# A multi-head latent attention with a gated FFN on one core: rope tables kept in SBUF, one copy of the keys, heads in turn, rope swap by ScalarE copies

## Chip, cores and metric

The kernel runs on one core of a Trainium2 chip. The metric is the device time of one execution in microseconds (us), the median of several runs. TensorE (PE), VectorE (DVE), ScalarE (ACT) and GpSimd (POOL) each run their own instruction stream in order; SyncE (SP) issues the DMAs. Semaphores tie the streams together. The whole program is written out by hand, so nothing but the order of the code sets the order on an engine.

## What is computed

```python
x = L0_attn_x                                    # (1, 2048, 256), float32
xn = layernorm(x)
s = attn(xn, ...)                                # 16 heads, causal, 2048 x 2048
g = silu(ffn(xn, ...))                           # gate and up 704 x 256, down 256 x 704
out = x + s * g

# attn: NOPE, ROPE, VD, LORA = 128, 64, 128, 64
q_nope, q_pe = split(x @ wq)                     # per head 128 + 64
ckv, k_pe = split(x @ wkv_a)                     # 64 + 64
ckv = rmsnorm(ckv) * kv_norm_scale
k_nope, v = split(ckv @ wkv_b)                   # per head 128 + 128
q_pe, k_pe = rope(q_pe), rope(k_pe)              # [x1*cos - x2*sin, x2*cos + x1*sin], halves of 32
scores = (concat(q_nope, q_pe) @ concat(k_nope, k_pe).T) * 192 ** -0.5, causal
out = softmax(scores) @ v, heads side by side, @ wo
```

## The kernel before

**Form.** The products of weights are folded, so that queries and keys have 128 rows: 64 of the latent space and 64 of rope. Keys are then the same for all heads. Float32 accuracy comes from splitting each operand into a high and a low part and adding three products (hi x hi, hi x lo, lo x hi). Queries (QA, QB for the two heads of a pair), keys (KA, KB) and x lie transposed in SBUF, each as hi and lo, 2048 columns. Head A has its rope rows on partitions 0 to 63 and its latent rows on 64 to 127, head B the other way round, so there are two copies of the keys.

**Units.** The 16 heads go as 8 pairs. A pair has 16 units (PU), a unit u does one head and two query tiles of 128 rows, tile 15 - k and tile k, against all keys at or below the diagonal: 17 key tiles whatever k is. It falls into three pieces m: m = 0 the first 1024 keys of the high tile, m = 1 the rest of the high tile, m = 2 the low tile. Before, head A has units 0 to 7 of a pair and head B units 8 to 15.

**One unit, by engine.** PE computes scores(u, m) into five banks of PSUM (s_ps, one set only); DVE takes the row maxima; ACT the exponentials (prob) and the high half of them in 16 bits (hl); the low half is made by POOL for m = 0 (`prob_low`, named low(u)) and by DVE for m = 1, 2. SP then issues two DMA transposes, turn_first(u) for m = 0 and turn_rest(u) for m = 1, 2, which turn hi and lo from hl into pT; PE multiplies pT by the values two units later (weigh, LAG = 2) and DVE normalises. In one turn of the loop PE does scores(u+1, 0), scores(u+1, 1), weigh(u-2, 0), scores(u+1, 2), the rest of weigh, and the jobs of u. ACT does exp(u, 0), exp(u, 1), hi(u, 0), exp(u, 2), the jobs of u-1, hi(u, 1), hi(u, 2). DVE normalises u-3, takes the maxima (u+1, 0) and (u+1, 1), does the jobs of u-1, low (u, 1) and (u, 2), and the maximum (u+1, 2). POOL does low(u) and then the steps of u. The waits: a score bank is free once its exponential is done; prob0 is single, so exp(u+1, 0) waits for low(u); hi(u) waits for the transpose of u-2.

**Jobs and steps.** The tables JOBS_*, with at most two jobs a unit, say at which unit PE, ACT and DVE do the small work of the pair itself, of the pair before (projection outT, outP) and of the next one: wqT, wkvT and wabs make the folded weights, `pe{g}` the rope rows of both heads for group g of 512 queries (PE 6 matmuls, ACT a copy into q_pe), `lat{g}` the latent rows of both heads (PE 6 matmuls, ACT two copies QA_hi, QB_hi, DVE two subtractions). POOL_* place POOL's steps: rope{g}.0 multiplies q_pe by cosT, rope{g}.1 q_swap by sinT, rope{g}.2 adds; then the sides A{g}hi, A{g}lo, B{g}hi, B{g}lo go into the query tiles. wpe_hi, wpe_lo and wkvs prepare weights. Groups go in the order 3, 0, 2, 1.

**SP's queue.** In order: turn_first(u), then, where they fall, `swap(g)` (four DMAs of 32 rows that write q_pe with its halves exchanged into q_swap), `load_tables` (cosT and sinT of the next group, 128x512 each; SBUF holds one group), turn_rest(u), and at k = 0, 11 the loads of the next pair's weights (wq_sb and wkvs, wo_sb).

## Time and profile before

| | us |
|---|---|
| median of 3 runs (1116.97 to 1122.3) | 1118.76 |
| profiled execution | 1120.68 |
| its span in the profile | 1118.9 |
| PE, DVE, ACT, POOL busy | 985.6, 831.2, 714.0, 662.8 |
| first transposes of pairs 0, 1, 7; of the last unit | 79.5, 208.7, 898.3; 997.4 |

The span is the time from the first to the last instruction. The attention runs from the setup (to about 70 us) to about 1007 us, the FFN fills the rest. The page gives busy time by engine, the chain that ended last and groups of instructions; stretches of time can be asked for by themselves, and so can the waits of one engine for another. An instruction of a DMA queue is an issue: the transfer lands some us later. A busy PE isn't a PE at its peak, since matmuls overlap.

### The profile page before, as it was taken

The numbers are of one execution on the slowest core, as the hardware profiler recorded it, in microseconds if no ns is written. First come the engines' busy times: TensorE is split into PE (matmuls) and PEld (weight loads), VectorE is DVE, ScalarE is ACT, GpSimd is POOL, SyncE is SP. The second block draws the span as 40 slices with busy tenths as digits, with TensorE's granted clock in tenths as the row PEclk, the third lists the DMA queues.
The fourth block names the chain that finished last, engine by engine and source line by source line (L and its number), as shares of the span: only waits on it lengthen the run. The fifth ranks groups of instructions, "written<-read, shape, count | busy, mean of one in ns | idle before, by whom it ended". The sixth has DMA issues, their size and how long they took to land.

```text
span 1118.9 us, 26420 instructions
## 1 busy us (share of the span) xinstructions
PE 985.6 (88%) x10576; PEld 842.8 (75%) x10576; DVE 831.2 (74%) x1359; ACT 714.0 (64%) x1033; POOL 662.8 (59%) x448
## 2 busy tenths in 40 slices
PE   6864898989988988999889998998899986989998
PEld 5743787778777877788778877876688775878887
DVE  6674687988787877878798779887888885873134
ACT  1335567776676767677677677776677774863232
POOL 3736766766576675756685658565857684422331
PEclk7777899999999999899999999999999998999999
DMA  5118899999999999999999999999999899992001
GB/s 146 38 40 168 152 186 197 197 197 184 184 187 199 189 187 185 202 184 188 189 207 185 197 190 206 180 192 178 202 178 211 179 192 207 178 176 76 1 20 57
DMA packets 600042, 184.92 MB, mean 165 GB/s; under 512 B 574960, under 2 KB 586864, under 8 KB 599920
## 3 DMA queue, kind: packets, MB, share of 16 engines
q1 hardware_dynamic: 595440, 182.57, 89.6%
q8 instruction: 84, 1.38, 0.5%
q10 hardware_dynamic: 4480, 0.66, 0.4%
q14 instruction: 38, 0.31, 0.1%
HBM read 30.09 MB, written 2.10 MB: 29 GB/s over the span
## 4 chain that ended last, share of the span: by engine, by line
PE 34%; DMA 24%; DVE 17%; POOL 10%; SPq 6%; ACT 5%; issue 4%; ACTq 1%; POOLq 0%
DMA pT<-hl 19%; PE s_ps L637 12%; PE s_ps L535 9%; DVE hl L948 5%; PE slot_ps L535 5%; DVE part_max L939 5%; POOL hl L1099 5%; ACT hl L743 3%; DMA sinT<-sinT_dram 2%; SPq L464 2%; ACT prob L809 2%; PE o_ps L653 2%; SPq L477 2%; PE o_ps L535 2%; PE o_ps L654 2%
## 5 line engine op out<-in xcount | busy, mean ns | idle before, releaser
L1099 POOL TENSOR_TENSOR hl<-prob,hl 128x1024 f16<-128x1024 f32 x128 | 274.5, 2144 | 228.3 <-ACT hl L743 224.4
L743 ACT ACTIVATE hl<-prob 128x1024 f16<-128x1024 f32 (+7 forms) x384 | 295.9, 804 | 160.3 <-DMA pT<-hl 159.6
L809 ACT ACTIVATE prob<-s_ps,neg_max 128x1024 f32<-128x1024 f32 (+7 forms) x384 | 316.7, 859 | 101.4 <-DVE neg_max L942 46.6
L939 DVE TENSOR_REDUCE part_max<-s_ps 128x1 f32<-128x1024 f32 (+7 forms) x256 | 243.7, 985 | 93.4 <-PE s_ps L637 74.4
L948 DVE TENSOR_TENSOR hl<-prob,hl 128x1024 f16<-128x1024 f32 (+7 forms) x256 | 255.9, 1035 | 62.4 <-ACT hl L743 62.1
L653 PE MATMUL o_ps<-v,pT 128*128 128x65 f16 x2176 | 231.8, 194 | 51.0 <-DMA pT<-hl 39.3
L653 PEld LDWEIGHTS o_ps<-v,pT 128*128 128x128 f16 x2176 | 205.4, 97 | 58.0 <-DMA pT<-hl 45.9
L654 PE MATMUL o_ps<-v,pT 128*128 128x64 f16 x2176 | 232.2, 196 | 0.0
L655 PE MATMUL o_ps<-v,pT 128*128 128x65 f16 x2176 | 231.1, 193 | 0.0
L655 PEld LDWEIGHTS o_ps<-v,pT 128*128 128x128 f16 x2176 | 205.6, 100 | 0.0
L654 PEld LDWEIGHTS o_ps<-v,pT 128*128 128x128 f16 x2176 | 204.8, 98 | 0.0
L637 PE MATMUL s_ps<-KA_hi,QA_hi 128*128 128x512 f32 (+3 forms) x320 | 129.0, 403 | 36.6 <-ACT prob L809 21.1
L637 PE MATMUL s_ps<-KB_hi,QB_hi 128*128 128x512 f32 (+3 forms) x320 | 125.0, 391 | 6.8 <-ACT prob L809 6.7
L637 PE MATMUL s_ps<-KA_lo,QA_hi 128*128 128x512 f32 (+3 forms) x320 | 120.7, 377 | 0.0
L637 PE MATMUL s_ps<-KA_hi,QA_lo 128*128 128x512 f32 (+3 forms) x320 | 120.2, 376 | 0.0
L637 PE MATMUL s_ps<-KB_hi,QB_lo 128*128 128x512 f32 (+3 forms) x320 | 117.4, 367 | 0.0
L637 PE MATMUL s_ps<-KB_lo,QB_hi 128*128 128x512 f32 (+3 forms) x320 | 117.3, 367 | 0.0
L637 PEld LDWEIGHTS s_ps<-KA_hi,QA_hi 128*128 128x128 f32 x320 | 63.3, 198 | 56.1 <-ACT prob L809 30.2
L937 DVE TENSOR_REDUCE neg_max<-s_ps 128x1 f32<-128x128 f32 (+7 forms) x128 | 95.4, 745 | 11.8 <-PE s_ps L640 11.8
L1231 POOL TENSOR_TENSOR hid_lo<-hid,hid_hi 128x512 fp32r<-128x512 f32 x24 | 31.4, 1307 | 75.5 <-ACT hid_hi L743 75.5
L637 PEld LDWEIGHTS s_ps<-KB_hi,QB_hi 128*128 128x128 f32 x320 | 60.8, 190 | 19.7 <-ACT prob L809 9.9
L1099 POOL TENSOR_TENSOR q_swap<-q_swap,sinT 128x512 f32<-128x512 f32 x32 | 45.1, 1409 | 47.1 <-DMA q_swap<-q_pe 45.7
(196 smaller groups left out, 1985.5 us busy)
## 6 DMA issues: line engine op xcount, KB each, us to landing
cosT<-cosT_dram SPq DMA_DIRECT2D x32, 256.0 KB, 4.0
sinT<-sinT_dram SPq DMA_DIRECT2D x32, 256.0 KB, 4.1
q_swap<-q_pe SPq DMA_DIRECT2D x128, 64.0 KB, 2.1
pT<-hl SPq DMA_TRANSPOSE x256, 5.2
wq_sb<-in_L_attn_wq_dram SPq DMA_DIRECT2D x8, 384.0 KB, 3.9
acc<-in_L_attn_x_dram SPq DMA_DIRECT2D x4, 512.0 KB, 6.5
wo_sb<-in_L_attn_wo_dram SPq DMA_DIRECT2D x8, 256.0 KB, 3.7
x_in<-in_L_attn_x_dram SPq DMA_DIRECT2D x1, 2048.0 KB, 8.5
```

Of the source, the lines that this page charges most:

```text
L535: last = nc.tensor.matmul(out_ap, a, b, start=(i == 0), stop=(i == n - 1))
L637: mm = nc.tensor.matmul(s_ps[:, b, 0:c], a[head][:, q], kk[head][:, k0 + c0:k0 + c0 + c], start=(j == 0), stop=(j == 2 and not ends))
L653: nc.tensor.matmul(whole, pT[:, b, :], v[:, kb, 0:LORA + 1], start=(m != 1 and b == 0), stop=False)
L654: nc.tensor.matmul(part, pT[:, b, :], v[:, kb, LORA + 1:VW], start=False, stop=False)
L655: last = nc.tensor.matmul(whole, pT[:, n + b, :], v[:, kb, 0:LORA + 1], start=False, stop=(m > 0 and b == n - 1))
L743: return nc.scalar.activation(dst, src, ACT.Copy)
L809: nc.scalar.activation(prob_of(u, m), score_bank(u, m), ACT.Exp, bias=neg_max[:, r:r + 1]).then_inc(exp_done, 1)
L937: nc.vector.tensor_reduce(neg_max[:, r:r + 1], src, AX.X, ALU.max, negate=True).then_inc(max_ready, 1)
L939: nc.vector.tensor_reduce(part_max[:, u % 2, m:m + 1], src, AX.X, ALU.max).then_inc(part_done, 1)
L948: nc.vector.tensor_tensor(both[:, w:2 * w], prob_of(u, m), both[:, 0:w], ALU.subtract).then_inc(lo_dve, 1)
L1099: return lambda: nc.gpsimd.tensor_tensor(dst, a, b, op)
L1231: nc.gpsimd.tensor_tensor(hid_lo[:, n % 2, it, :], hid[:, j % 2, :], hid_hi[:, n % 2, it, :].bitcast(F32), ALU.subtract).then_inc(hid_lo_d ...
```

## The change

- **Tables.** cosT and sinT become 128x2048 and are loaded once, in four parts, in the setup. TABLES_AT and the reloads go.
- **Rows.** Both heads have rope rows on 0 to 63 and latent rows on 64 to 127, so one copy of the keys (K_hi, K_lo) does, with 4 key jobs in the setup in place of 8. The weights for both parts lie in one tile, wc_hi, wc_lo.
- **Query jobs.** `q{A,B}{g}` takes the place of `pe{g}` and `lat{g}`: one job for each head and group, again 6 matmuls. ACT makes four copies of its result: rope rows into q_pe, the two halves of 32 rows in exchanged order into q_swap, latent rows into the queries. The swap DMAs go. DVE makes one low part a job.
- **Rope.** For head B the last addition moves to DVE (`rope_of_b`, from partitions 64 to 127 into pe_b on 0 to 63); POOL's covers head A alone. q_pe and q_swap get two buffers.
- **Heads in turn.** Unit u has head u % 2 and step k = u % 16 // 2; groups 3 and 0 serve units 0 to 7 of a pair, 2 and 1 units 8 to 15. The normalised output goes into o_tiles, two buffers of four tiles. All job and step tables are written anew.
- **Setup.** qA3, qB3, qA0, qB0 replace pe3, pe0, lat3, lat0; POOL does B3 and B0 before the first unit.

```diff
 def head_of(u):
-    return u // HALF % 2
+    return u % 2
-JOBS_BEFORE = {0: ["outP0a", "outP0b"], 1: ["outT1"], 3: ["outP1a", "outP1b"], 4: ["outT2"], 6: ["outP2a", "outP2b"],
-               7: ["outT3"], 9: ["outP3a"], 10: ["outP3b"]}
-JOBS_OWN = {10: ["wvo"], 14: ["outT0"]}
-JOBS_NEXT = {2: ["wqT"], 5: ["pe3"], 7: ["wkvT"], 8: ["pe0"], 9: ["wabs"], 11: ["pe2", "lat3"], 12: ["lat0"], 13: ["pe1"],
-             14: ["lat2"], 15: ["lat1"]}
+JOBS_BEFORE = {2: ["outT3"], 4: ["outP3a", "outP3b"]}
+JOBS_OWN = {0: ["qA2"], 1: ["qB2"], 2: ["qA1"], 3: ["qB1"], 5: ["wvo"], 6: ["outT0"], 7: ["outP0a", "outP0b"], 10: ["outT1"],
+            12: ["outP1a", "outP1b"], 14: ["outT2"], 15: ["outP2a", "outP2b"]}
+JOBS_NEXT = {3: ["wqT"], 5: ["wkvT"], 6: ["wabs"], 8: ["qA3"], 9: ["qB3"], 10: ["qA0"], 11: ["qB0"]}
...
-POOL_NEXT = {2: ["wpe_hi"], 3: ["wpe_lo"], 4: ["wkvs"], 7: rope(3)[:2], 8: [rope(3)[2], "A3hi"], 9: ["A3lo"], 10: rope(0)[:2],
...
+POOL_NEXT = {1: ["wkvs"], 6: ["wpe_hi"], 7: ["wpe_lo"], 10: rope(3)[:1], 11: rope(3)[1:] + ["A3hi"], 12: ["A3lo", rope(0)[0], "B3hi"],
...
-                for name in jobs_at(u - 1):
-                    if name[0].startswith("pe"):
-                        swap(int(name[0][2:]), name[1])
-                if u in TABLES_AT:
-                    load_tables(*TABLES_AT[u])
...
-                    copy(QA_hi[LORA:P, c], ps[LORA:P, :])
-                    copy(QB_hi[0:LORA, c], ps[0:LORA, :]).then_inc(hi_done, 1)
-                    copy(q_pe[:], ps).then_inc(act_freed, 1)
+                    n = group_no(g, pair)
+                    if n >= 2:
+                        before = GROUP_ORDER[(n - 2) % NG], (n - 2) // NG
+                        act.wait_ge(pool_done, POOL.after((f"rope{before[0]}.2", before[1])))
+                        act.wait_ge(rope_b, n - 1)
+                    half = ROPE // 2
+                    copy(q_pe[h * ROPE:(h + 1) * ROPE, n % 2, :], ps[0:ROPE, :])
+                    copy(q_swap[h * ROPE:h * ROPE + half, n % 2, :], ps[half:ROPE, :])
+                    copy(q_swap[h * ROPE + half:(h + 1) * ROPE, n % 2, :], ps[0:half, :])
+                    copy(queries(Q_hi, h, g)[ROPE:P, :], ps[ROPE:P, :]).then_inc(hi_done, 1)
...
+                nc.vector.tensor_tensor(pe_b[:, n % 2, :], pe[ROPE:P, n % 2, :], q_swap[ROPE:P, n % 2, :], ALU.add).then_inc(rope_b, 1)
```

On SP's queue, in pair 0 before (hl0 and pT0 belong to turn_first, hl12 and pT12 to turn_rest):

```order
L470 DMA_TRANSPOSE pT0<-hl0 128x16x128
L464 DMA q_swap<-q_pe 32x512 x4
L477 DMA_TRANSPOSE pT12<-hl12 128x18x128
L470 DMA_TRANSPOSE pT0<-hl0 128x16x128
L477 DMA_TRANSPOSE pT12<-hl12 128x18x128
L470 DMA_TRANSPOSE pT0<-hl0 128x16x128
L451 DMA cosT<-cosT_dram 128x512
L452 DMA sinT<-sinT_dram 128x512
L477 DMA_TRANSPOSE pT12<-hl12 128x18x128
```

and now, at the change from pair 0 to pair 1:

```order
L446 DMA_TRANSPOSE pT0<-hl0 128x16x128
L453 DMA_TRANSPOSE pT12<-hl12 128x18x128
L416 DMA wq_sb<-in_L0_attn_wq_dram 128x2x384
L417 DMA wkvs<-in_L0_attn_wkv_b_dram 64x512
L446 DMA_TRANSPOSE pT0<-hl0 128x16x128
L453 DMA_TRANSPOSE pT12<-hl12 128x18x128
L446 DMA_TRANSPOSE pT0<-hl0 128x16x128
L453 DMA_TRANSPOSE pT12<-hl12 128x18x128
```

Between two transposes there is nothing left but the loads of weights. On ACT, one turn of the loop in pair 0 before, with the jobs pe2 and lat3 of the next pair in it:

```order
L809 ACTIVATE prob12<-s_ps,neg_max 128x512
L743 ACTIVATE hl0<-prob0 128x1024
L809 ACTIVATE prob12<-s_ps,neg_max 128x640
L743 ACTIVATE q_pe<-slot_ps 128x512
L743 ACTIVATE QA_hi<-slot_ps 64x512
L743 ACTIVATE QB_hi<-slot_ps 64x512
L743 ACTIVATE hl12<-prob12 128x512
L743 ACTIVATE hl12<-prob12 128x640
```

and now, with the query job of one head (QB21 holds head B's groups 2 and 1):

```order
L772 ACTIVATE prob12<-s_ps,neg_max 128x896
L706 ACTIVATE hl0<-prob0 128x1024
L772 ACTIVATE prob12<-s_ps,neg_max 128x256
L706 ACTIVATE q_pe<-slot_ps 64x512
L706 ACTIVATE q_swap<-slot_ps 32x512 x2
L706 ACTIVATE QB21_hi<-slot_ps 64x512
L706 ACTIVATE hl12<-prob12 128x896
L706 ACTIVATE hl12<-prob12 128x256
```

The exchanged copies stand between exp(u, 2) and the two halves of the unit, and such a block now comes in eight units of a pair. On POOL the scaling of the next pair's wkvs stood five low halves behind the pair's start; now it stands right behind the second:

```order
L1080 TENSOR_TENSOR hl0<-prob0,hl0 128x1024 x2
L1080 TENSOR_TENSOR wkvs<-wkvs,scale_sb 64x512
L1080 TENSOR_TENSOR hl0<-prob0,hl0 128x1024
L1080 TENSOR_TENSOR pe<-q_pe,cosT 128x512
L1080 TENSOR_TENSOR hl0<-prob0,hl0 128x1024
```

The load of wkvs is issued by SP behind turn_rest of the pair's unit 0, as before.

## Rows read from the trace of the kernel before

**Rows 1.** Stretches: start:end, length, busy us and instructions (x) by engine.
```profile
core 0: us, PE busy (x) PEld busy (x) DVE busy (x) ACT busy (x) POOL busy (x), PEclk, DMA share, GB/s
79.50:208.70 129.20, 105.70 (x1141) 89.51 (x1140) 91.23 (x145) 87.06 (x124) 84.66 (x57) 0.89 0.93 176
208.70:898.30 689.60, 629.83 (x7357) 534.69 (x7355) 568.07 (x903) 499.09 (x709) 455.24 (x282) 0.98 1.07 191
961.90:997.30 35.40, 34.42 (x480) 30.50 (x478) 33.13 (x62) 30.84 (x47) 12.89 (x7) 1.00 1.21 191
```
**Rows 2.** Timeline of SP's queue, pair 4: start us, duration us, issue.
```profile
576.36 1.94 SPq L470 DMA_TRANSPOSE pT<-hl  x1
578.39 4.01 SPq L477 DMA_TRANSPOSE pT<-hl  x1
582.50 1.80 SPq L470 DMA_TRANSPOSE pT<-hl  x1
...
594.12 1.76 SPq L470 DMA_TRANSPOSE pT<-hl  x1
595.97 3.06 SPq L464 DMA_DIRECT2D q_swap<-q_pe  x4
...
601.95 3.14 SPq L470 DMA_TRANSPOSE pT<-hl  x1
```
**Rows 3.** Timeline of POOL, same place: the low half low(68).
```profile
575.60 2.15 POOL L1099 TENSOR_TENSOR hl<-prob,hl 128x1024 f16<-128x1024 f32 x1
```
**Rows 4.** Waits, 208.7 to 898.3 us: total us, times, longest.
```profile
ACT hl L743 <- DMA pT<-hl: 140.7, 78, 4.7
...
POOL q_swap L1099 <- DMA q_swap<-q_pe: 37.7, 11, 4.4
```
**Rows 5.** The page's DMA issues: count, KB each, median us to landing.
```profile
wkvs<-in_L_attn_wkv_b_dram SPq DMA_DIRECT2D x8, 128.0 KB, 3.9
```
**Rows 6.** Groups by shape on ACT, 208.7 to 898.3 us: busy us, mean ns | idle before.
```profile
L743 ACT ACTIVATE QA_hi<-slot_ps 64x512 fp32r<-64x512 f32 x24 | 14.2, 593 | 1.3 <-PE slot_ps L535 0.8
...
L743 ACT ACTIVATE q_pe<-slot_ps 128x512 f32<-128x512 f32 x24 | 14.2, 591 | 0.2 <-PE slot_ps L535 0.2
```
**Rows 7.** Timeline of ACT in the setup: copies in a row.
```profile
51.46 0.58 ACT L743 ACTIVATE KB_hi<-s_ps 128x512 fp32r<-128x512 f32 x1
51.94 0.59 ACT L743 ACTIVATE KA_hi<-s_ps 128x512 fp32r<-128x512 f32 x1
```
**Rows 8.** Groups by shape on DVE, 208.7 to 898.3 us.
```profile
L948 DVE TENSOR_TENSOR hl<-prob,hl 128x512 f16<-128x512 f32 x24 | 30.4, 1268 | 6.3 <-ACT hl L743 6.3
...
L896 DVE TENSOR_TENSOR QB_lo<-slot_ps,QB_hi 64x512 fp32r<-64x512 f32 x24 | 16.4, 682 | 0.3
```
**Rows 9.** Timeline of SP's queue, end of pair 7.
```profile
961.96 3.14 SPq L470 DMA_TRANSPOSE pT<-hl  x1
...
970.19 2.97 SPq L477 DMA_TRANSPOSE pT<-hl  x1
...
997.36 1.99 SPq L470 DMA_TRANSPOSE pT<-hl  x1
```
**Rows 10.** Timeline of POOL, same place: low(123).
```profile
970.68 2.15 POOL L1099 TENSOR_TENSOR hl<-prob,hl 128x1024 f16<-128x1024 f32 x1 [3.49 <-ACT hl L743]
```
**Rows 11.** Groups on POOL, 208.7 to 898.3 us.
```profile
L1099 POOL TENSOR_TENSOR pe<-q_pe,cosT 128x512 f32<-128x512 f32 x24 | 31.5, 1313 | 25.1 <-DMA sinT<-sinT_dram 23.6
...
L1099 POOL TENSOR_TENSOR wkvs<-wkvs,scale_sb 64x512 f32<-64x512 f32 x6 | 8.3, 1388 | 0.5
```
**Rows 12.** Timeline of ACT, end of pair 7: exp(124, 0), in brackets idle time before.
```profile
974.15 1.11 ACT L809 ACTIVATE prob<-s_ps,neg_max 128x1024 f32<-128x1024 f32 x1 [1.25 <-DVE neg_max L942]
```
**Rows 13.** Timelines of POOL and DVE in the setup.
```profile
40.94 1.28 POOL L1099 TENSOR_TENSOR pe<-q_pe,cosT 128x512 f32<-128x512 f32 x1 [1.15 <-issue]
...
67.25 0.67 DVE L886 TENSOR_TENSOR KA_lo<-s_ps,KA_hi 128x512 fp32r<-128x512 f32 x1
```
**Rows 14.** Waits, 79.5 to 208.7 us.
```profile
PE s_ps L637 <- POOL QA_lo L1099: 11.4, 1, 11.4
```
**Rows 15.** Waits of the whole span, at the load of the FFN weights.
```profile
POOL up_raw L1099 <- DMA down_scale<-in_L_ffn_down_s_dram: 13.3, 1, 13.3
```

280 lines of the change are left out of this document (129 added, 151 removed).

## Prediction

> **What bounds the kernel now.** I read the stretches first, then the queue of SyncE, then who waits for whom, then the durations.
>
> The stretches [rows 1] cut the span at the first transposes of head pairs 0, 1 and 7. Pairs 1 to 6 (96 units, a unit being one head and two query tiles) take 689.6 us, 7.18 us a unit or 114.9 us a pair. In them DVE is busy 568.07 us (5.92 a unit), ACT 499.09 (5.20), POOL 455.24 (4.74), PE 629.83 (6.56). PE's figure is too high as a floor: its records last longer than the distance to the next start, so each tail of a group counts. No engine is full, the DMA share is 1.07.
>
> SyncE's queue [rows 2] shows what is full. From 576.36 to 594.12 us it issues only transposes, back to back, three units in 17.76 us or 5.92 a unit. The next unit has four swaps in the queue (3.06 us) and takes 601.95 - 594.12 = 7.83 us. GpSimd had the low halves of the unit whose first transpose starts at 582.50 ready at 575.60 + 2.15 = 577.75 [rows 3]: the transpose is 4.7 us late, with everything computed. So the queue is behind, and the swaps and table loads stand in it. The waits agree [rows 4]: ACT, which may not overwrite a half before the transpose of two units earlier has landed, waits 140.7 us for that in pairs 1 to 6; GpSimd waits 37.7 us for swaps and 23.6 us for tables [rows 4, 11]. **The in-order DMA path sets the pace of the attention, and every engine trails it.**
>
> **Removed from the queue.** Per pair four loads of cosT and of sinT, and four times four swaps; they stand in eight of its 16 units. The unit with swaps was 1.9 us longer than the three without. If every one of the eight units a pair with swaps or tables costs 1.9 to 2.3 us, that is 15 to 18 us a pair; 16 x 5.92 = 94.7, plus 2 to 3 us for the two loads that stay, gives a DMA path of 97 to 98 us a pair after the change. That is the fastest a pair can be. Of each table 28 of 32 loads go, and all 128 swaps; four loads of each remain in the setup.
>
> **Added on ScalarE.** Before, a query group costs three copies (q_pe, QA_hi, QB_hi), after it eight (for each head q_pe, two of 32 rows, and the upper half of the queries). That is 5 more a group, 20 a pair. A copy of 512 columns takes 591 ns [rows 6], and copies in a row start 0.48 us apart [rows 7]; the columns, not the rows, are the same in 128- and 64-row copies (591 and 593 ns), and I take the 32-row ones as equal. So 20 x 0.48 to 0.59 = 9.6 to 11.8 us a pair; ACT goes from 499.09/6 = 83.2 to 93 to 95 us a pair. It sits between exp(u, 2) and the halves (u, 1), (u, 2), in 8 of 16 units. Behind it on ACT stand those halves, behind them DVE's low parts and the second transpose, and the next unit's exponentials. [...]
>
> **Added on VectorE.** One addition a group (rope_of_b, 64x512, two SBUF inputs), 4 a pair. The nearest rows [rows 8] are a subtraction of the same size with one input in PSUM, 682 ns, and the low part of 512 columns with both inputs in SBUF, 1268 ns on average. I take 1.0, 4.0 us a pair, with 2.7 and 5.1 us as ends. The query low parts stay two a group. DVE goes from 568.07/6 = 94.7 to 98.7 us a pair. The Trainium skill (SBUF — State Buffer, Who interferes with whom) says why the two rows may differ: an operation of VectorE with two SBUF inputs and one of GpSimd that reads SBUF exclude each other, the later waits. By it every addition would meet GpSimd and cost 1.3 us: 1.2 us a pair more than I count, 1054 in place of the forecast.
>
> **GpSimd.** The same steps with the same shapes. Its waits for swaps and tables (61.3 us in pairs 1 to 6) go; they were slack. What is new: the scaling of wkvs moves from step 4 to step 1 of a pair, right behind low(1), while its load is still issued behind the second transpose of unit 0. The load lands 3.9 us after its issue [rows 5], and stands behind the issue of wq (some 0.6 us). In the free stretch at the end the second transpose of a unit has been issued at 970.19 + 2.97 = 973.16, and the next unit's low half ends at 970.68 + 2.15 = 972.83 [rows 9, 10]. So GpSimd stands 0.3 + 0.6 + 3.9 = 4.8 us, then scales for 1.4 [rows 11]: 6.2 us, where a unit of 6.6 us leaves 6.6 - 2.15 = 4.4 beside the low half. low(2), and behind it the overwriting of prob0 by exp(3, 0), come 1.8 us late. From 972.83 to the exponential that needed it at 974.15 there was 1.3 us of slack [rows 10, 12]; I count 1 us a pair, between 0 and 3.
>
> **TensorE.** Six matmuls of 512 columns a job, two jobs a group, as before (per head now, where it was rope and latent). The order of heads changes which tiles come when, and not how many. The queries of groups 2 and 1 are now wanted from unit 8 of a pair, not from unit 4.
>
> **What a pair then takes.** The stretch from 961.90 to 997.30 us [rows 1] is the kernel without swaps, tables and next pair's work. First transposes start at 961.96 and 997.36 [rows 9], with six units between them, 5.90 us each. DVE is busy 33.13 of 35.4 us there, 94%, PE 97%. So the engines can be packed to 94% of DVE when the DMA path isn't behind. 98.7 / 0.936 = 105.4; with 1 us for wkvs, **106 us a pair**, 6.6 a unit. ACT is then 89% busy and the DMA path has 8 us a pair to spare. From PE's side: 629.83/6 = 105.0 us with its tails, 108 at 97%, an upper bound that fits.
>
> **Setup, first and last pair.** In the setup the rope of group 3 starts at 40.94 us [rows 13]. Now it needs the job of both heads, which waits for wabs, after two kv jobs; GpSimd stands about 10 us and then has rope (3 x 1.3), two key blocks, rope again before DVE can end, where it ended at 67.25 + 0.67 us [rows 13]. Against that stand four key jobs, with their copies, which go. I take +3 us, between 0 and +8. Pair 0 took 129.2 us; its one long hole is PE waiting 11.4 us for QA_lo [rows 14], because group 2 was wanted at unit 4. Now it has until unit 8. Pair 0 at 106: -23. Pair 7 (99 us before) gets the four jobs of its own groups 2 and 1 and some output jobs from the end, about +4; the hole at the load of the FFN weights, where GpSimd waited 13.3 us [rows 15], gets a unit more of lead, about -3. Together +1. The FFN stage I leave as it is.
>
> **Sum.** 1118.9 + 3 - 23 - (689.6 - 636) + 1 = 1046 us of span. The profiled execution was 1120.68 us, 1.8 over its span and 1.9 over the median of 1118.76; so 1046 also stands for the median of the runs.
>
> **The rivals.**
> (A) The forecast, 1046, DVE and PE near full: 0.52.
> (B) The engines pack tighter and the DMA path stays the bound at 98 us a pair. Seven pairs at 8 us less: 1046 - 56 = 990. For: half the units carry light jobs, and buffers are two deep. Against: DVE would be 98.7/98, over full. Only with 0.68 us additions and shorter low parts does it come near, so 0.08, and then nearer to 1005.
> (C) ScalarE bound in its eight full units. ACT's work in a unit is about 83.2/16 = 5.2, less the old copies (12 x 0.48 a pair, 0.36), so 4.8 without any group work; four copies make 6.8, with an outT or wqT copy 7.3, and waits for neg_max (1.25 us before an exponential in the free stretch, [rows 12]) on top. Eight units at 7.6, eight at 6.2: 110 us a pair. 1046 + 7 x 4 = 1074. For: the scores have one set of banks, so what delays an exponential delays the next scores. Against: ACT can run ahead of DVE by the two buffers of its halves. 0.28.
> (D) No change, 1119: the swaps and tables were hidden and the transposes' own rate sets 7.2 us. The 5.92 us stretch excludes it nearly: 0.03.
> (E) Slower. The loop exp -> scores -> maximum -> exp already needs 5.9 us, and the copies, which stand in it on ACT, are not absorbed at all, with q jobs on PE waited for as well. It decides from (114.9 - 8 x 6.1)/8 = 8.3 us for a unit with a query job. At 8.5 (5.9 + 4 x 0.59 and 0.25 of waits) a pair has 117: pairs 1 to 6 +12, pair 0 -12, pair 7 +9, setup +3: 1119 + 12 = 1131. 0.05. A worse tail of C, between 1085 and 1113, has the remaining 0.04.
>
> **How the numbers follow.** Forecast 1046. The range goes from 1005 (B at its likely end) to 1086 (C with a pair at 111.5). A measurement of this kernel can tell about 0.5% from no change. Faster by over 0.5% (under 1113): A, B, C and the tail, 0.92; within 0.5%: D, 0.03; slower: E, 0.05.
>
> **What would show it.** The SyncE queue should have no table load or swap after the setup, and a transpose should start within 1 us of its low part in most units; ACT's wait for pT should fall from 140.7 us to under 40. First transposes of pairs should stand 106 us apart, DVE over 90% busy, ACT near 89%. If ACT is the bound, DVE's waits for ACT hl grow and units with four copies are 1 us and more longer than the others. GpSimd should wait for wkvs once a pair, 3 to 5 us. First transpose of pair 0 near 82 us, the next pair's near 188. Wrong it would be if the transposes alone, with the queue free of the rest, still ran at 7 us a unit, or if ACT waited for PE's query jobs in each of the eight units.

## The result, and the profile after

| | before | after |
|---|---|---|
| median of four runs each | 1117.87 us (1115.93 to 1122.30) | 1132.87 us (1127.33 to 1133.82) |
| ratio to before, 95% interval | | 1.012 (1.009 to 1.015) |
| the profiled execution, its span | 1120.68, 1118.9 us | 1133.82, 1132.0 us |

The changed kernel is 1.2% slower. The forecast was 1046 us, the range ended at 1086; both are wrong, and so is the sign. The number that came out is the one that the prediction gave to its rival E, 1131 us at 117 us a pair; whether for E's reasons is told below. Single executions that took over 1.5% longer than the fastest of the same kernel (one each of d1, d2 and e1, the last at a granted clock of 0.555 and 1511.8 us) are left out of every median and ratio.

The stretches of the changed kernel, cut at the first transposes of pairs 0, 1 and 7 as in [rows 1] (start:end, length, busy us and instructions by engine, granted clock, DMA share, GB/s):

```profile
core 0: us, PE busy (x) PEld busy (x) DVE busy (x) ACT busy (x) POOL busy (x), PEclk, DMA share, GB/s
88.40:202.80 114.40, 103.02 (x1131) 86.21 (x1130) 97.80 (x146) 94.34 (x137) 77.29 (x47) 0.95 0.96 162
202.80:904.00 701.20, 625.65 (x7322) 528.86 (x7322) 617.59 (x925) 568.73 (x828) 455.28 (x282) 0.99 0.94 161
904.00:1010.30 106.30, 92.53 (x1149) 79.34 (x1149) 91.44 (x148) 83.55 (x121) 60.58 (x35) 0.95 1.01 177
```

The first transpose comes at 88.4 us (79.5 before). Pair 0 takes 114.4 us (129.2). Pairs 1 to 6 take 701.2 us, 116.9 a pair (689.6, 114.9). DVE is busy 102.9 us a pair where it was 94.7, ACT 94.8 where it was 83.2. GpSimd is as before. The DMA share has fallen from 1.07 to 0.94.

Who waits for whom, whole span (us in total, times, longest):

```profile
POOL hl L1080 <- ACT hl L706: 253.0, 103, 7.5
ACT prob L772 <- DVE neg_max L910: 112.2, 78, 3.9
...
ACT prob L772 <- DVE neg_max L915: 63.9, 35, 13.6
...
PE o_ps L617 <- DVE o_tiles L933: 58.1, 40, 2.6
...
POOL wkvs L1080 <- issue: 17.9, 4, 5.8
...
ACT hl L706 <- DMA pT<-hl: 6.1, 2, 5.8
...
POOL up_raw L1080 <- DMA down_scale<-in_L_ffn_down_s_dram: 6.0, 1, 6.0
```

The wait that bounded the old kernel, ACT for landed transposes [rows 4], is gone: 140.7 us in pairs 1 to 6 alone, now 6.1 us in the whole span. In its place ScalarE waits for VectorE's maxima, and TensorE for VectorE's o_tiles. The page's chain of work that ended last says the same:

```profile
DVE 27%; PE 25%; ACT 21%; issue 14%; POOL 8%; DMA 2%; SPq 1%; ACTq 1%; POOLq 0%
```

SyncE's queue has gaps now. Over pairs 1 to 6 its issues fill 509 of 701 us, where they filled 658 of 690. A few of them (start us, duration us):

```profile
455.31 2.56 SPq L453 DMA_TRANSPOSE pT<-hl  x1
458.26 1.93 SPq L446 DMA_TRANSPOSE pT<-hl  x1
463.11 2.68 SPq L453 DMA_TRANSPOSE pT<-hl  x1
465.88 2.94 SPq L446 DMA_TRANSPOSE pT<-hl  x1
471.09 2.40 SPq L453 DMA_TRANSPOSE pT<-hl  x1
```

Between the end of one issue at 460.19 and the next start at 463.11 it waits for a low part. By the trace's start and end times a unit's first transpose now starts 0.9 us behind its low half on average, and 67 of 96 start within 1 us; before it was 4.5 us, and 1 of 96. Against [rows 2], where transposes stood back to back, the queue has been freed, as the prediction said. What happens instead in this place is on ScalarE and VectorE. ScalarE, from one exponential of unit 52 to the next of unit 53, 7.99 us, with idle time before in brackets:

```profile
460.38 1.91 ACT L772 ACTIVATE prob<-s_ps,neg_max 128x1024 f32<-128x1024 f32 x2
462.17 1.05 ACT L706 ACTIVATE hl<-prob 128x1024 f16<-128x1024 f32 x1
463.70 0.58 ACT L772 ACTIVATE prob<-s_ps,neg_max 128x384 f32<-128x384 f32 x1 [0.48 <-DVE neg_max L910]
464.31 0.59 ACT L706 ACTIVATE q_pe<-slot_ps 64x512 f32<-64x512 f32 x1
464.91 1.18 ACT L706 ACTIVATE q_swap<-slot_ps 32x512 f32<-32x512 f32 x2
466.11 0.59 ACT L706 ACTIVATE QB_hi<-slot_ps 64x512 fp32r<-64x512 f32 x1
466.73 0.60 ACT L706 ACTIVATE wqT<-slot_ps 128x512 f32<-128x512 f32 x1
467.22 1.25 ACT L706 ACTIVATE hl<-prob 128x768 f16<-128x768 f32 x2
468.37 1.90 ACT L772 ACTIVATE prob<-s_ps,neg_max 128x1024 f32<-128x1024 f32 x2
```

Four copies of a query job run from 464.31 to the start of the next at 466.73: 2.42 us, 0.60 apart and not 0.48 as the full-height copies of [rows 7]. VectorE at two pairs of low parts over the same 1152 columns, and GpSimd at the second:

```profile
452.69 2.01 DVE L921 TENSOR_TENSOR hl<-prob,hl 128x896 f16<-128x896 f32 x2 [0.28 <-ACT hl L706]
...
460.07 3.00 DVE L921 TENSOR_TENSOR hl<-prob,hl 128x896 f16<-128x896 f32 x2 [0.28 <-ACT hl L706]
```
```profile
459.67 1.28 POOL L1080 TENSOR_TENSOR pe<-pe,q_swap 64x512 f32<-64x512 f32 x1
461.03 1.77 POOL L1080 TENSOR_TENSOR QA_hi<-pe,ones 64x512 fp32r<-64x512 f32 x1
```

The second pair has GpSimd's steps beside nearly all of it (from 460.07 to 462.80, and it ends at 463.07) and takes 3.00 us; GpSimd's own step takes 1.77 us there, where the same form took 1.03 at its least. The cost of GpSimd to VectorE's low parts, which the prediction had only inside one average (1268 ns, [rows 8]), turned out to be one of the main terms (a3, d3 and f1 below).

### The profile page after: what moved, and what is told of

Its sections match the earlier page's. It is cut to its first block, busy times and chain, and to the rows that moved or that the text cites. A ratio compares the mean times of both kernels' runs of the same rounds, so it can differ in the third digit from the quotient of the medians.

```text
span 1132.0 us, 26361 instructions
## 1 busy us (share of the span) xinstructions
PE 985.5 (87%) x10560; PEld 838.2 (74%) x10560; DVE 896.3 (79%) x1383; ACT 806.2 (71%) x1189; POOL 666.9 (59%) x448
## 4 chain that ended last, share of the span: by engine, by line
DVE 27%; PE 25%; ACT 21%; issue 14%; POOL 8%; DMA 2%; SPq 1%; ACTq 1%; POOLq 0%
DVE hl L921 12%; PE s_ps L503 9%; PE s_ps L601 8%; ACT hl L706 7%; ACT prob L772 6%; DVE part_max L912 5%; ACT q_swap L706 4%; DVE neg_max L910 4%; POOL hl L1080 4%; PE slot_ps L503 3%; DVE acc L884 2%; PE o_ps L503 2%; ACT q_pe L706 2%; DVE pe_b L869 1%; DMA scale_sb<-_attn_kv_norm_scale_dram 1%
## 5 line engine op out<-in xcount | busy, mean ns | idle before, releaser
L921 DVE TENSOR_TENSOR hl<-prob,hl 128x768 f16<-128x768 f32 (+7 forms) x256 | 280.1, 1133 | 6.4 <-ACT hl L706 4.3
L601 PE MATMUL s_ps<-K_hi,QA_hi 128*128 128x512 f32 (+3 forms) x320 | 129.1, 403 | 25.0 <-ACT prob L772 17.3
L601 PE MATMUL s_ps<-K_hi,QB_hi 128*128 128x512 f32 (+3 forms) x320 | 126.6, 396 | 14.1 <-ACT prob L772 14.0
L601 PE MATMUL s_ps<-K_hi,QA_lo 128*128 128x512 f32 (+3 forms) x320 | 119.9, 375 | 0.0
L601 PE MATMUL s_ps<-K_lo,QA_hi 128*128 128x512 f32 (+3 forms) x320 | 119.6, 374 | 0.0
L601 PE MATMUL s_ps<-K_hi,QB_lo 128*128 128x512 f32 (+3 forms) x320 | 119.3, 373 | 0.0
L601 PE MATMUL s_ps<-K_lo,QB_hi 128*128 128x512 f32 (+3 forms) x320 | 118.6, 371 | 0.0
L910 DVE TENSOR_REDUCE neg_max<-s_ps 128x1 f32<-128x256 f32 (+7 forms) x128 | 96.2, 752 | 1.9
L601 PEld LDWEIGHTS s_ps<-K_hi,QA_hi 128*128 128x128 f32 x320 | 62.3, 195 | 46.9 <-ACT prob L772 30.6
L706 ACT ACTIVATE q_swap<-slot_ps 32x512 f32<-32x512 f32 x122 | 71.7, 588 | 1.4
```

The source lines that it names most:

```text
L601: mm = nc.tensor.matmul(s_ps[:, b, 0:c], a[:, q], kk[:, k0 + c0:k0 + c0 + c], start=(j == 0), stop=(j == 2 and not ends))
L706: return nc.scalar.activation(dst, src, ACT.Copy)
L910: nc.vector.tensor_reduce(neg_max[:, r:r + 1], src, AX.X, ALU.max, negate=True).then_inc(max_ready, 1)
L921: nc.vector.tensor_tensor(both[:, w:2 * w], prob_of(u, m), both[:, 0:w], ALU.subtract).then_inc(lo_dve, 1)
```

## The experiments

Theory V: VectorE is the bound of the changed kernel, through its additions and through low parts slowed by GpSimd. Theory S: ScalarE's copies are. A third possibility is that the floor under both, 106 us a pair, was itself wrong. All times below are medians, with the ratio to the kernel before measured beside them and its 95% interval; "a pair" is the distance of the first transposes of pairs 1 and 7 by six, from the trace of one execution. Rows of stretches have the columns of the first table above.

### One or the other addition taken away

a1_no_add: VectorE's addition over 8 columns.

```diff
-nc.vector.tensor_tensor(pe_b[:, n % 2, :], pe[ROPE:P, n % 2, :], q_swap[ROPE:P, n % 2, :], ALU.add)
+nc.vector.tensor_tensor(pe_b[:, n % 2, 0:8], pe[ROPE:P, n % 2, 0:8], q_swap[ROPE:P, n % 2, 0:8], ALU.add)
```

> The changed kernel with VectorE's new addition (rope_of_b) over 8 columns in place of 512, so the rope rows of head B are left out (they stay the zeros of a memset in the setup); all waits and all other instructions stay. Theory V (VectorE is the bound of the changed kernel: the additions and low parts slowed by GpSimd): 4 additions of 1.23 us a pair go, 32 in all = 39 us, nearly all on the path, so 1095 to 1100 us. Theory S (ScalarE's copies are the bound in the units with query jobs): VectorE only follows, 1125 to 1133 us.

Measured: 1101.6 us, 0.979 (0.977 to 0.982), a pair 112.6 us.

a2_no_swap_copies: ScalarE's exchanged copies over 8 columns.

```diff
-copy(q_swap[h * ROPE:h * ROPE + half, n % 2, :], ps[half:ROPE, :])
-copy(q_swap[h * ROPE + half:(h + 1) * ROPE, n % 2, :], ps[0:half, :])
+copy(q_swap[h * ROPE:h * ROPE + half, n % 2, 0:8], ps[half:ROPE, 0:8])
+copy(q_swap[h * ROPE + half:(h + 1) * ROPE, n % 2, 0:8], ps[0:half, 0:8])
```

> The changed kernel with the second eviction in exchanged order (four copies of 32 rows a query group, 16 a pair) over 8 columns in place of 512; the sine part of the rope is left out with it, all waits stay. 16 x 0.60 us = 9.6 us a pair go, less what an 8-column copy still takes (some 0.2 us each), so about 6.5 us a pair or 50 us in all. Theory S: most of it is on the path, 1080 to 1095 us. Theory V: VectorE stays full, and at most 10 us go, 1122 to 1133 us.

Measured: 1100.0 us, 0.978 (0.974 to 0.982), a pair 112.9 us.

a3_neither: both edits.

> Both edits at once: VectorE's addition and ScalarE's exchanged copies over 8 columns each. What is left is the changed kernel's order with its free SyncE queue and nothing added. If one of the two theories holds alone, this gives what its own run gives. If the two engines take turns as the bound (the units with copies by ScalarE, the others by VectorE), it gives more than the sum of both: under 1060 us. If the order of work itself (GpSimd's steps three to a unit, jobs in rows of units, keys and heads taking turns) costs what the prediction missed, it stays above 1090 us.

Measured: 1070.6 us, 0.951 (0.948 to 0.954), a pair 109.2 us.

Neither theory holds alone, and a3 lies between the cases written down for it (under 1060, over 1090). From the changed kernel (116.9) a1 takes 4.3 us a pair, a2 4.0 and both together 7.7: they nearly add up. The narrowed instructions are not gone. An exchanged copy over 8 columns still took 0.17 us, so ScalarE's busy time over pairs 1 to 6 fell from 568.7 to 528.7 us in a2, 6.7 a pair, and 4.0 of it were on the path. An addition over 8 columns took 0.45 us on average where the full one took 1.15 (1.21 in pairs 1 to 6), and VectorE's busy time fell from 617.6 to 601.3 us in a1, 2.7 a pair: less than the 4.3 that the pair gained.

How that can be is seen in unit 7 of a pair (counted from 0), which gives half of it: between its first exponential and that of unit 8 the changed kernel takes 8.7 us (mean of six), a1 6.5. VectorE and ScalarE there, in pair 3 of the changed kernel:

```profile
481.99 1.58 DVE L869 TENSOR_TENSOR pe_b<-pe,q_swap 64x512 f32<-64x512 f32 x1
483.60 3.67 DVE L921 TENSOR_TENSOR hl<-prob,hl 128x640 f16<-128x640 f32 x2
487.19 0.68 DVE L910 TENSOR_REDUCE neg_max<-s_ps 128x1 f32<-128x512 f32 x1
```
```profile
487.90 0.69 ACT L772 ACTIVATE prob<-s_ps,neg_max 128x512 f32<-128x512 f32 x1 [3.50 <-DVE neg_max L910]
```

The maximum that the last exponential of unit 7 waits for stands on VectorE behind the addition and behind the low parts of unit 6, and these take 3.67 us beside GpSimd. ScalarE stands 3.5 us; in a1 it stands 1.3 us at this place.

The same distances show where the copies count. The eight units of a pair that hold a query job's copies take 7.46 us on average and the other eight 7.15. With the exchanged copies narrowed (a2) they take 6.93 and 7.18, with the additions narrowed (a1) 7.46 and 6.61. Each edit shortened one half of the units, which is why the two nearly add up. The prediction's signs of a full ScalarE are missing: units with four copies should have been 1 us and more longer than the others, and are 0.3 us longer; VectorE's waits for ScalarE's high parts (DVE hl <- ACT hl) should have grown, and fell from 52.9 to 3.4 us over pairs 1 to 6.

What remains in a3, 109.2, is still over the predicted 106; 2.1 us a pair of additions and 2.6 of small copies are left in it.

### The old kernel with its queue freed

b1_free_queue: the kernel before with the tables of group 3 loaded once for all groups, the swaps left out, and q_pe in the place of the swapped rows.

```diff
-                    run((name, pair), tt(q_swap[:], q_swap[:], sinT[:], ALU.mult), (swapped, 64 * (n + 1)))
+                    run((name, pair), tt(q_swap[:], q_pe[:], sinT[:], ALU.mult))
...
-                for name in jobs_at(u - 1):
-                    if name[0].startswith("pe"):
-                        swap(int(name[0][2:]), name[1])
-                if u in TABLES_AT:
-                    load_tables(*TABLES_AT[u])
```

> The kernel before with its SyncE queue freed and nothing put in its place: the tables are loaded once (so later groups take the wrong ones) and the four swaps are left out, GpSimd multiplying q_pe by the sine table with the same shape. If the in-order DMA path alone set its pace, as the prediction has it, a pair falls from 114.9 to about 101 to 106 us and the time to 1045 to 1065 us. If the engines were right behind the queue, at 7 us a unit, it gives 1095 to 1117 us.

Measured: 1056.0 us, 0.939 (0.935 to 0.942), a pair 105.3 us. The first half of the prediction stands: the swaps and loads in the DMA path held the old kernel, and without them a pair is 9.6 us shorter. The stretch of pairs 1 to 6 and the chain of this kernel:

```profile
200.90:832.80 631.90, 608.15 (x7324) 522.49 (x7320) 552.52 (x901) 498.15 (x709) 442.69 (x283) 0.99 1.04 178
```
```profile
PE 54%; DVE 25%; POOL 6%; ACT 5%; issue 5%; DMA 3%; SPq 1%; ACTq 1%; POOLq 0%
```

PE is busy 96% (608.15 of 631.90) and holds 54% of the chain, DVE is busy 87%. So TensorE is the fullest engine here, but 105.3 us a pair is not its floor: f1 below leaves TensorE's work as it is and takes 102.8 us a pair. From the other side, TensorE's matmuls at the median distance between their starts (0.23 us for 512 columns of scores, 0.03 us for the products with the values) come to 96 to 97 us a pair in this kernel, in f1 and in the changed one alike: an estimate from the traces' start times. No run changed TensorE's own work. The changed kernel has PE busy 89% (625.65 of 701.20) and 25% of the chain: it waits more for the other engines.

### GpSimd's steps beside VectorE

d3_less_pool: a3 with GpSimd's 16 split steps a pair over 8 columns from pair 1 on.

```diff
+                m = 8 if pair else BANK
-                src = (pe_b if head else pe)[0:ROPE, n % 2, :]
-                hi, lo = queries(Q_hi, head, g)[0:ROPE, :], queries(Q_lo, head, g)[0:ROPE, :]
+                src = (pe_b if head else pe)[0:ROPE, n % 2, 0:m]
+                hi, lo = queries(Q_hi, head, g)[0:ROPE, 0:m], queries(Q_lo, head, g)[0:ROPE, 0:m]
```

> The changed kernel without its addition and exchanged copies (1070.6 us, 109.2 us a pair), with the 16 split steps of GpSimd a pair over 8 columns in place of 512 from pair 1 on (so these pairs keep old rope rows in most columns). In the changed order GpSimd has three steps behind its low half in 12 of 16 units, and the long units are those. If these runs of steps, through the late low half or through slower low parts of VectorE, are what the changed order costs against the kernel before with a free queue (105.3 us a pair), a pair falls to 105 us or less, 1035 to 1045 us. If it is the extra copy and the small ones on ScalarE, or the order of the jobs, a pair stays at 108 to 109 and the time at 1060 to 1070 us.

Measured: 1040.4 us, 0.928 (0.924 to 0.932), a pair 104.8 us. The two kernels, a3 first, each with all engines and then with the low and high halves (hl) alone, where the busy times are those of DVE, ACT and POOL:

```profile
189.20:844.20 655.00, 607.84 (x7322) 522.12 (x7321) 602.26 (x925) 528.17 (x828) 462.36 (x282) 1.00 1.02 173
```
```profile
189.20:844.20 655.00, 215.79 (x192) 222.21 (x288) 214.58 (x96) 1.00 1.02 173
```
```profile
187.70:816.60 628.90, 609.11 (x7322) 524.13 (x7322) 558.80 (x925) 528.43 (x828) 357.54 (x282) 0.99 1.05 180
```
```profile
187.70:816.60 628.90, 174.45 (x192) 222.34 (x288) 211.25 (x96) 0.99 1.05 180
```

Nothing was taken from VectorE, and its busy time fell by 43.5 us; the low parts (the first figure of the hl rows, DVE) give 41.3 of it. PE is back at 97%. The other way in which GpSimd's steps could cost time, a late low half of its own, did not change: ScalarE's wait for it over pairs 1 to 6 was 11.6 us in a3 and is 13.4 us, while its waits for VectorE's maxima fell from 111.1 to 82.7 us. So work on GpSimd is work on VectorE here. The expectation counts three steps of GpSimd in 12 of 16 units of the changed order; by its step tables it is 8 of 16, against 4 in the old order. Sorting the pairs of low parts of the changed kernel by whether GpSimd ran beside them (from the trace's start and end times, pairs 1 to 6): 36 with GpSimd beside under a tenth of their time took 1.50 us (the two durations added), 12 with GpSimd beside over nine tenths 3.23 us; in a3, 30 took 1.50 and 31 took 3.05.

The same narrowing in the old order: e1_less_pool_before.

> The kernel before with its queue freed (1056.0 us, 105.3 us a pair, wrong tables), with GpSimd's 16 split steps a pair over 8 columns from pair 1 on. In the changed order the same edit gave 4.4 us a pair and took VectorE's low parts from 215.8 to 174.5 us over pairs 1 to 6. If GpSimd's steps cost the same wherever they stand, a pair falls to 101 us and the time to 1028 to 1032 us. If the old order has them where VectorE doesn't meet them, or where the loop is bound otherwise, a pair stays above 103.5 us: 1045 to 1056 us, and the order is what the changed kernel pays for.

Measured: 1039.1 us, 0.926 (0.922 to 0.931), between the two cases. Its trace is that of the execution of 1511.8 us, so the same kernel was traced again as f1_less_pool_before:

> The kernel before with its queue freed and GpSimd's split steps over 8 columns from pair 1 on, once more for its trace. The times gave 14.6 us less than with full steps, about 2.3 us a pair: 103 us. If the steps cost less in the old order because VectorE meets them less, the low parts over pairs 1 to 6 fall from 184.4 us by 10 to 20 us, where they fell by 41.3 in the changed order; if they fall by 40 us here too, it is the loop that does not profit, not the meeting.

One run, 1043.3 us, a pair 102.8 us:

```profile
200.30:817.00 616.70, 605.28 (x7323) 520.11 (x7320) 520.20 (x900) 496.69 (x709) 341.63 (x283) 1.00 1.09 183
```
```profile
200.30:817.00 616.70, 151.20 (x192) 221.94 (x289) 206.31 (x96) 1.00 1.09 183
```

The low parts fell from 184.4 to 151.2 us, by 33 where the changed order gave 41: my 10 to 20 us were wrong, GpSimd meets VectorE nearly as much in the old order. The time gained is 2.5 us a pair against 4.4, and f1 is a single execution. A reading that fits is that the old order has less to gain: PE is busy 98% here, and ScalarE waits for landed transposes again (22.9 us over pairs 1 to 6, 25 times). It was not tested. What the changed order costs is visible in a3 against b1: low parts 215.8 against 184.4 us, with the same GpSimd steps at other places, 30 us more on ScalarE (four full copies a pair more, and the sixteen narrowed ones), and 12.7 us of narrowed additions on VectorE. Together these cost 3.9 us a pair; how the 3.9 divide among them wasn't separated.

### Mending the changed kernel

c1_add_on_pool: head B's addition as a fourth step of GpSimd's rope.

```diff
+                else:
+                    run((name, pair), tt(pe_b[:, n % 2, :], pe[ROPE:P, n % 2, :], q_swap[ROPE:P, n % 2, :], ALU.add))
```

> The changed kernel with head B's rope addition on GpSimd (a fourth step of a group's rope) in place of VectorE; nothing is left out. VectorE loses 32 additions of 1.15 us (37 us), GpSimd gains 32 steps of 1.3 us (42 us) and is busy 63% instead of 59%. With the addition narrowed away the time was 1101.6 us. If what counts is the work on VectorE, this gives 1100 to 1110 us; if more work on GpSimd slows VectorE's low parts as much (both read SBUF), it gives 1115 to 1133 us.

Measured: 1105.8 us, 0.985 (0.981 to 0.989), a pair 113.2 us. It is 3.7 us a pair better than the changed kernel, and the first that leaves nothing out and beats the kernel before. The low parts went up from 213.8 to 225.7 us, 2 us a pair, which is the part of the additions that comes back through GpSimd.

c2_consts_first: table loads held behind the constants.

```diff
+            sp.wait_ge(consts_loaded, 64)
             for g in GROUP_ORDER:
                 load_tables(g)
```

> The changed kernel with SyncE waiting for the four constants before it issues the eight table loads; nothing is left out. In the setup VectorE waited 8.3 us for scale_sb where it had waited 4.3, and the first transpose came at 88.4 where it had come at 79.5. If the 2 MB of tables in front of the constants delay them, the first transpose comes 4 us earlier or more and the time is 1124 to 1129 us. If the setup is late through GpSimd's later start of the ropes alone, nothing changes: 1133 us.

Measured: 1124.3 us (ten runs), 1.003 (1.000 to 1.006). The first transpose comes at 78.6 us, where it was 88.4. The row it goes back to, of the changed kernel, is VectorE's first operation on a constant, and the wait before it:

```profile
20.58 0.29 DVE L991 CAST wkva_hi<-wkva_sb 128x256 fp32r<-128x256 f32 x1 [8.27 <-DMA scale_sb<-_attn_kv_norm_scale_dram]
```

It is 2.9 us in c2. So 2 MB of tables issued ahead delayed the constants; holding them back makes the setup 9.8 us shorter, 5.4 of them in this wait.

f2_pool_and_consts: both.

> The changed kernel with head B's addition on GpSimd and with the table loads behind the constants; nothing is left out. One gave 0.985 of the kernel before, where the changed kernel has 1.012, the other 1.003. One acts in every pair and the other in the setup, so they should add up: 0.974 to 0.980, 1092 to 1098 us. If the setup's gain only moves a wait into pair 0, 0.983 to 0.987.

Measured: 1103.9 us, 0.981 (0.977 to 0.985). They do not add up: 0.985 went to 0.981 and not to 0.976, and the intervals overlap, so it isn't shown that f2 is faster than c1 at all. c1 alone had its first transpose at 84.8, f2 has it at 84.1. VectorE's wait for scale_sb is 3.0 us here and 8.3 in c1, so the constants do come earlier, and the first transpose gains 0.7 us by it. VectorE waits 3.4 us for GpSimd's pe in both; that GpSimd's longer ropes now end the setup fits this, but wasn't tested.

### Other ways to take the swaps off the queue

c3_swap_copies: the kernel before, with the exchanged copies in its old order (q_swap with two buffers), tables still loaded for each group.

```diff
+                    for i in range(4):
+                        copy(q_swap[i * half:(i + 1) * half, n % 2, :], ps[(i ^ 1) * half:(i ^ 1) * half + half, :])
                     copy(q_pe[:], ps).then_inc(act_freed, 1)
```

> The kernel before with ScalarE's four copies of 32 rows in place of the four swaps by DMA, and everything else of it (order of heads, two copies of the keys, tables loaded again for each group); nothing is left out. Without swaps and reloads it took 1056 us. 16 copies of 0.60 us a pair are 9.6 us; in the changed kernel 53 us of such copies cost 33 us, so 72 us cost some 45 us: 1095 to 1105 us, with 0 to 10 us more if the table loads still hold the queue back. If the copies are absorbed as the prediction had it, 1060 to 1075 us.

Measured: 1086.9 us, 0.967 (0.963 to 0.970), a pair 109.2 us. Between the two cases that were expected, and 3.3% faster than the kernel before with this one part of the change. ScalarE does nearly as much as in the changed kernel (554.2 us over pairs 1 to 6 against 568.7), yet its pairs are 7.7 us shorter.

c4_shifted_products: the swap inside GpSimd's product with the sine; GpSimd's steps are placed anew for it.

```diff
+                elif i < 5:
...
+                    a, b = slice((i - 1) * half, i * half), slice((i - 1 ^ 1) * half, (i - 1 ^ 1) * half + half)
+                    run((name, pair), tt(q_swap[a, :], q_pe[b, n % 2, :], sinT[b, :], ALU.mult))
```

> The kernel before with the swap done inside GpSimd's product with the sine table: four products of 32 rows that read one block of rows and write its neighbour, in place of four DMAs and one product of 128 rows; nothing is left out. No copy and no DMA is added; GpSimd gets 12 more steps of 1.3 us a pair (125 us in all, 650 to 775 us busy, 73%). Base is 1056 us, plus 0 to 10 us for the table loads and 8 us for pair 0. If GpSimd has the room that its waits show and VectorE isn't slowed, 1062 to 1080 us. If its steps slow VectorE's low parts, or three steps a unit delay the low halves, 1085 to 1110 us.

Measured: 1090.5 us, 0.970 (0.967 to 0.974), a pair 108.3 us, at the edge of the slower case. No work was added to VectorE, and its low parts rose to 241.2 us over pairs 1 to 6 (184.4 in b1): 9.5 us a pair. ScalarE now waits 77.1 us for GpSimd's low half over the same stretch, where it waits 3.1 us in c3. Twelve products a pair on GpSimd and sixteen copies a pair on ScalarE cost about the same.

d1_tables_by_pool and d2_tables_by_act: c3 with the table loads issued on GpSimd's or on ScalarE's queue.

```diff
+                    if 2 <= n < NG * PAIRS - 1:
+                        nxt = query_cols(GROUP_ORDER[(n + 1) % NG])
+                        pool.wait_ge(pool_done, POOL.after((name, pair)))
+                        pool.dma_start(cosT[:], cosT_in[:, nxt]).then_inc(tables_more, 16)
+                        pool.dma_start(sinT[:], sinT_in[:, nxt]).then_inc(tables_more, 16)
```

> The version with swap copies in the old order (1086.9 us), with the table loads of groups 3 and later issued by GpSimd itself, right behind the product that used the old table; nothing is left out. In that version the four units of a pair with table loads took 7.7, 7.9, 8.6 and 8.0 us where the kernel with the free queue took 5.8, 6.3, 7.5 and 6.8, and the units with swap copies took no longer. If the loads' places in SyncE's queue are what is left, a pair falls from 109.2 to about 105.5 us and the time to 1058 to 1068 us. If it is the copies, 1080 to 1087 us stay.

> The same, with these loads issued on ScalarE's queue behind exp(u, 2); nothing is left out. An issue there took 0.50 us in the setup, eight a pair are 4 us of ScalarE. If ScalarE absorbs this as it absorbs the swap copies in this order, 1060 to 1070 us; if its time counts in full, 1080 to 1095 us.

Measured: 1115.6 us, 0.994 (0.991 to 0.997), a pair 113.6 us, and 1087.9 us, 0.968 (0.962 to 0.975), a pair 110.4 us. Neither helps, and the first costs 29 us. GpSimd's issue, and SyncE's queue at the same place:

```profile
213.97 0.59 POOL L1113 DMA_DIRECT2D cosT<-cosT_dram  x1 [0.30 <-POOL q_swap L1083]
214.55 0.55 POOL L1114 DMA_DIRECT2D sinT<-sinT_dram  x1
```
```profile
213.95 4.96 SPq L459 DMA_TRANSPOSE pT<-hl  x1
219.01 7.55 SPq L466 DMA_TRANSPOSE pT<-hl  x1
226.65 1.91 SPq L459 DMA_TRANSPOSE pT<-hl  x1
```

The two transposes that meet the loads hold the queue for 12.5 us, where the mean of such a pair over pairs 1 to 6 of c3 is 2.48 + 3.19 = 5.7. This place is one of the worst: three of the trace's 128 pairs of transposes are over 12 us, and the mean in d1 is 2.69 + 3.31 = 6.0. The loads are off SyncE's queue, but not out of the transposes' way. The Trainium skill (DMA: Bandwidth & Descriptors, Issuing engines are not separate DMA queues) says that DMAs of all issuing engines run on the same 16 DMA engines and interleave; these rows agree, and on GpSimd's queue it was worse than in order. How the 29 us divide between longer transposes and GpSimd's own issues (1.1 us a group) wasn't separated.

e3_small_tables: c3 with the loads over 8 columns from the second group of pair 1 on, at the same places.

> The version with swap copies in the old order (1086.9 us), with the table loads from the second group of pair 1 on over 8 columns (so the rope there uses old columns): the same issues at the same places of the queue, 8 KB in all in place of 512 KB. If the bytes are what costs (512 KB beside transposes), a pair falls from 109.2 to 105.5 to 106.5 us and the time to 1062 to 1068 us. If the issues and their order among the transposes cost, it stays at 1080 to 1087 us.

Measured: 1079.0 us, 0.962 (0.957 to 0.966), a pair 108.4 us. The bytes are worth 0.7 us a pair at most (the intervals of e3 and c3 overlap), not the 3 to 4 that would have brought it to b1. The four units with loads became 0.8 to 1.1 us shorter each, and units with copies longer by up to 1.1 us. It looks as if loads and copies each hid part of the other in c3. With the bytes gone, the copies and the issues of the loads that remain cost 3.1 us a pair over b1 (108.4 against 105.3); these two weren't separated.

### The best version

e2_first_splits_early: c3, with pair 0's first four split steps in the setup.

> The version with swap copies in the old order (1086.9 us), with the four split steps of head B for pair 0 moved into the setup, where GpSimd waits 16 us for the first halves; nothing is left out. Pair 0 took 126.7 us where the others took 109.2. Four steps of 1.1 to 1.4 us come off the road to group 2's queries: 5 us less, 1080 to 1084 us. If they delay the first low half instead, 1087 to 1090 us.

Measured: 1083.2 us, 0.965 (0.962 to 0.968). e4_one_table_load: one load for both tables on top.

> The version with the early split steps, with one load of 512 KB for both tables in place of two of 256 KB; nothing is left out. The first load of a pair takes 1.1 us to issue, the second 0.44. If each load's own waiting among the transposes counts, 2 us a pair go: 1065 to 1072 us. If the bytes count, it stays at what the version with early split steps takes, within 3 us.

Measured: 1082.2 us, 0.965 (0.961 to 0.968). Both leave out nothing, and for e4 the second case of its expectation came, that one load is worth no more than two. Their intervals hold each other's value and c3's: neither edit is shown to be worth anything over c3. Pair 0 fell from 126.7 to 120.5 us in e2, but its setup ended 6.8 us later, so the time moved and did not go. The best that was found is 3.3 to 3.5% faster than the kernel before (c3, e2, e4), against 1.2% slower for the change.

## Why the prediction was wrong

**Right.** The bound of the kernel before: SyncE's in-order queue, shown by b1. That the change frees it: ACT's wait for pT from 140.7 to 6.1 us, and most first transposes within 1 us of their low half. The price of an addition by itself, 1.0 us taken, 1.15 measured. Pair 0's hole, PE for QA_lo [rows 14], is gone. GpSimd's stand before wkvs: 4.8 us were worked out, and over pairs 1 to 6 it stands 29.2 us before its six steps, 4.9 each (half of it is put down to the profile's "issue", half to ACT hl). Its price in time wasn't separated.

**Step "What a pair then takes".** The rule that the engines pack to 94% of DVE was wrong. With DVE at 94.7 us it gave 101.2 us a pair for b1, which measured 105.3 with DVE at 87%: 4.1 us of the error. In f1, with DVE at 86.7 us a pair, it gives 92.6; measured was 102.8, with PE at 98%. The same rows [rows 1] had PE at 34.42 of 35.4 us, 97%, and the prediction put that figure aside as too high to be a floor. The objection to it is sound (105.0 us of records before became 101.4 in b1 and 100.9 in f1 with the same matmuls), but the bound from PE's side, 108, was the nearer one, and it was waved through ("an upper bound that fits"). Of the 4.1 us, 2.5 go when GpSimd's steps are narrowed (f1); the rest stands with PE full.

**Step "Added on ScalarE".** The copies were priced about right in ScalarE's own time (10 to 12 us forecast, 94.8 - 83.2 = 11.6 found), and then counted at nothing in the pair, because ScalarE would be 89% busy. ScalarE is 81% busy (568.73 of 701.20), less than forecast, and yet its added time was on the path for 0.5 to 0.6 of it: of the 6.7 us a pair that narrowing takes off the exchanged copies, 3.4 us (a1 to a3) to 4.0 us (the changed kernel to a2). A reading that fits the unit lengths: the loop of exponential, scores, maximum and exponential passes through several engines in turn, and time added to one of them where the loop passes counts, whatever the engine's share of the span. Within it, the spacing of 0.48 us was that of full-height copies; the new ones are 0.60 apart.

**Step "Added on VectorE".** 4.0 us of additions were taken as 4.3 on the path (4.0 / 0.936). Narrowing them gave 4.3 too, but that is chance: the edit took only 2.7 us a pair off VectorE. The step lacked that the additions stand in front of the low parts and of a maximum, as unit 7 shows.

**Step "GpSimd. The same steps with the same shapes".** They are, but for rope's addition, now over 64 rows; and they stand elsewhere: three behind the low half in 8 of 16 units, where it was 4. a3 against b1 has 31 us more of low parts over pairs 1 to 6, and, with one full copy a group more on ScalarE and the narrowed ones, a pair 3.9 us longer. The prediction weighed the rule of the Trainium skill (SBUF — State Buffer, Who interferes with whom) for the additions alone, at 1.2 us a pair, and never asked what it does to the 32 low parts of a pair, each of which has two SBUF inputs. The traces agree with that rule: 1.50 us for a pair of low parts alone, 3.0 to 3.2 beside GpSimd in a3 and in the changed kernel.

**The sum of a pair.** Forecast: 101.2 (old work at 94% of DVE) + 0 (order, copies) + 4.3 (additions) + 1 (wkvs) = 106.5, put at 106. Measured: 105.3 (b1) + 3.9 (a3 over b1: the place of GpSimd's steps, the wait before wkvs, and what a3 keeps of copies and additions) + 7.7 (what narrowing takes of additions and exchanged copies) = 116.9.

**Setup.** +3 was taken, within 0 to +8, and it was +8.9. GpSimd's later ropes were foreseen; the eight table loads ahead of the constants stood in the diff and weren't priced. c2 gives 78.6 in place of 88.4 when they are held back, 0.9 under the kernel before: so the delay went with this term, which the prediction had at nothing.

**The whole.** The forecast and the top of the range follow from 106 and 111.5 us a pair (7 x 5.5 over 1046 is 1084.5; 1086 was put). 1132.0 - 1046 = 86 us: setup 5.9, pair 0 8.4 (114.4 where 106 was put), pairs 1 to 6 65.2, pair 7 and what follows 6.4 (rounded).

**The rivals.** E had the time and the pair (1131 and 117), and of its reasons one in part: that copies in the loop are not absorbed (it had them count in full, and they count by half). The rest was luck. It put units with a query job at 8.5 us and the others at 6.1; measured are 7.46 and 7.15. It had query jobs on PE waited for; ScalarE's waits for PE before q_pe come to 2.8 us in the whole span. And its setup was 6 us short where its pair 0 was 3 us long. C had units with copies right (7.6) and took the other eight for 6.2, with VectorE absorbing the rest; they are 7.15, through low parts beside GpSimd and through the additions. Neither allowed several engines to be late by turns, and that is what a1, a2 and the unit lengths show. B would need the queue as the bound, which ACT's 6.1 us excludes; D is excluded by b1. The chance of 0.05 for slower followed from treating each addition as either bound or free.

## What to carry to other kernels

When a queue is freed, every engine that was fairly full in a free stretch is a candidate for the next bound; here VectorE's 94% was taken as the rule, and TensorE's 97% was the nearer figure. In a loop that passes through all engines, work moved from a full queue to an engine with 20% idle time is not free. What a microsecond costs depends on where it stands: here 0.5 to 0.6 us for one on ScalarE beside the loop's exponentials, and more than 1 for one on VectorE in front of a maximum that ScalarE waits for. Look at unit lengths by kind before an average: 117 us a pair came out by two different sets of lengths. Price a part by itself before taking the whole: the exchanged copies in the old order alone gave 3.3%, the full change took it all back.
